# The last stage's product as three fp32r products, its operand split and stored as two halves

## The chip, the cores and the metric

One core of one Trainium2 chip runs the whole kernel in one launch. The metric is the time of one execution on the device in microseconds (us). Five engines work side by side, each through its own list of instructions in order, and wait for each other on semaphores: TensorE (PE in the profile, with PEld its weight loads), VectorE (DVE), ScalarE (ACT), GpSimd (POOL) and SyncE (SP), which here only starts transfers.

## The reference

All activations are float32, [2, 1024, 512]. Four blocks are added to `x` in turn:

```
x = x + attention_a(layernorm(x))     # 16 heads, filtered along time
x = x + ffn(layernorm(x))             # 8 experts of width 16, the best 2 of a softmax gate
x = x + attn_b(layernorm(x))
x = x + ffn(layernorm(x))             # the same weights again

def attn_b(X):
    h = layernorm(X) * ln_w + ln_b
    Q, K, V = split(h @ W_in + b_in)              # 512 each
    Q, K = rope(Q), rope(K)
    A = sum over time of (K / |K|) * V            # one row of 512 for each batch
    Y = A[:, None, :] * Q
    return Y @ W_out + b_out + X
```

The product of this document is `Y @ W_out`. Since `Y = A * Q`, the kernel forms `Q @ (diag(A) W_out)`: the 512x512 matrix `diag(A) W_out` is made once for each batch, when the sum over time is known.

## The kernel before

Three stages follow each other: `normalise`, `attention` and `tail`. Only `tail` is changed. The 2 x 1024 rows are cut into NT = 16 tiles of 128 rows (TB = 8 to a batch, KC = 4 blocks of 128 columns in 512).

`tail` is one software pipeline of 34 rounds, `for s in range(2 * NT + 2)`, written out for each engine in the order in which that engine runs it. In rounds 0 to 15 tile `t = s` of attention_a's output is multiplied with its weight and enters the first ffn; one to four rounds later the same tile passes through the ffn and attn_b's projections. In rounds 16 to 31 tile `s - 16` is multiplied with `diag(A) W_out` (`last_product`) and passes the second ffn. Rounds 16 to 19 hold both kinds of work, rounds 20 on only the second.

What one round does, with the lines of the profile:

- TensorE: transpose of the second norm of tile `s-3` (L1667); the product of tile `s` (L1594 through `product` for the first 16 tiles, L1650 for the last 16); transpose of the first norm (L1439) and of the gated hidden row (L1456); the experts down (L1448) and up (L1460); projections k and v (L1594); transpose of the rotated q of tile `s-4` into the PSUM bank `tq` (L1722); projection q (L1594). The transpose L1439 stands between the third and the fourth column block of `last_product`.
- VectorE: bias added to q (L1820); the low half of the second norm's transpose (`hTl`, L1826); the low half of the next input tile (`aTl`, L1745, up to round 14); `x`, the sum of the product and the residual (L1804), its statistics (L1353 to L1359); the first norm `n1` (L1374), which needs GpSimd's reciprocal root (L1363); the expert sum (L1411), its statistics; bias added to k (L1864); the gate (L1391 to L1403); the second norm `h2` (L1759); k times v (L1876); bias added to v (L1884). In rounds 13 and 21 the copy of A's columns (L1763) and four products `wout * acol` into `wab` (L1768) stand at the end (`columns`).
- GpSimd: rotation of q of tile `s-4` (L1998, L2000, L2001); the residual's bias (L2013) and its transfer to DRAM (L2015); the root for the first norm (L1363), and for the second (L2023); the root for |k| and the rotation of k; the sum over time (`summed`, L2038, or a copy L2035 at the first tile of a batch). In rounds 18 on it starts the output transfers (L2043).
- ScalarE: copies and casts out of PSUM (L1940, L1417, L1432, and the high half `aTh` L1929), the exponentials of the gate, the square of k (L1962), the residual for the last stage (L1972), the copy of `tq` into `qT` (L1981) and its transfer to DRAM (`qt_scratch`, L1983).
- SyncE: `load_tile`. For a tile of the last stage it loads the 256 KB of `qt_scratch` (L1548) and 256 KB of residual (L1550).

Up to round 19 a tile is loaded into one of two slots, from round 20 (`DEEP_AT`) into one of four, the other two of which are the buffers of q and k.

A projection is made of fp32r products: with operands x = xh + xl and w = wh + wl, `product` adds xh·wh, xl·wh and xh·wl (three matmuls for each of the four column blocks). `last_product` uses plain float32 operands, one matmul for each block, which shows in the trace as two instructions.

Of the kernel before, what the change touches and what calls it, by code (L numbers as in the profile page):

```python
# [237 lines left out]
def build(nc, a, out):  # L238
# [5 lines left out]
    qt_scr = nc.dram_tensor("qt_scratch", (NT, P, KC, P), F32, kind="Internal").ap()  # L244
    res_scr = nc.dram_tensor("res_scratch", (NT, P, E), F32, kind="Internal").ap()
    with ExitStack() as outer:
# [14 lines left out]
        with ExitStack() as ctx:  # L261
            def sb(name, shape, dt=F32):
# [4 lines left out]
                wab=place[:, 0:B * KC * E].rearrange("p (b c e) -> p b c e", b=B, c=KC),  # L267
# [1051 lines left out]
R = 4  # L1319
# [144 lines left out]
def tail(nc, a, x_tiles, out_tiles, att_scr, qt_scr, res_scr, w, late):  # L1464
    with ExitStack() as ctx:
# [8 lines left out]
        ident, wab, bout = w["ident"], w["wab"], w["bout"]  # L1474
# [6 lines left out]
        winh, winl = sb("winh", [P, KC, 3 * E], F32R), sb("winl", [P, KC, 3 * E], F32R)  # L1481
        aT = sb("aT", [P, 2, KC, P])
# [29 lines left out]
        s_res, s_fold2, s_col, s_acol, s_wab = (sem(n) for n in ("res", "fold2", "col", "acol", "wab"))  # L1512
# [4 lines left out]
        COLS_AT = (TB + 5, NT + 5)  # L1517
        DEEP_AT = NT + 4

        aTs = [aT[:, 0], aT[:, 1]] + [q[:, i].rearrange("p (c t) -> p c t", c=KC) for i in range(2)]  # L1520
# [5 lines left out]
        def loaded(t):  # L1526
            i = slot(t)
            uses = t // 2 if t < DEEP_AT else (DEEP_AT // 2 if i < 2 else 0) + (t - DEEP_AT) // R
            return s_in[i], 32 * uses + 32
# [6 lines left out]
        def _(sp):  # L1536
            def load_tile(t):
                if t >= DEEP_AT + R:
                    sp.wait_ge(ex.s_x, t - R + 1)
                elif t >= DEEP_AT + 2:  # L1540
                    sp.wait_ge(s_tq, NT)
                    sp.wait_ge(s_kv, NT)
                elif t >= 2:
                    sp.wait_ge(ex.s_x, t - 1)
                if t >= NT:
                    u = t - NT
                    sp.wait_ge(s_qTd[u % 2], u // 2 * 16 + 16)
                    sp.dma_start(aTs[slot(t)], qt_scr[u]).then_inc(s_in[slot(t)], 16)  # L1548
# [39 lines left out]
        def _(pe):  # L1588
# [53 lines left out]
            def last_product(s, rows):  # L1642
                if rows.start == 0:
                    pe.wait_ge(*loaded(s))
                    pe.wait_ge(s_wab, KC * ((s - NT) // TB + 1))
                    if s == DEEP_AT + 1:
                        pe.wait_ge(s_qb, NT)
                    pe.wait_ge(ex.s_x, s if wide(s) is wide(s - 1) else s - 1)
                for c in rows:
                    mm = mmul(wide(s)[:], aTs[slot(s)][:, c], wab[:, (s - NT) // TB, c], start=(c == 0), stop=(c == KC - 1))  # L1650
# [5 lines left out]
            for s in range(2 * NT + 2):  # L1656
# [12 lines left out]
                if NT <= s < 2 * NT:  # L1669
                    last_product(s, range(KC - 1))  # L1670
                if 0 <= s - 1 < 2 * NT:
                    ex.pe_turn(pe, s - 1, t0)
                if NT <= s < 2 * NT:
# [10 lines left out]
                elif s < NT:  # L1684
                    if s == WHOLE:
# [4 lines left out]
                            aTl[:, s % 2].rearrange("p c t -> p (c t)"), woh, wol, 0).then_inc(s_w, 1)  # L1690
                if s == 1:
# [25 lines left out]
                if 0 <= t < NT:  # L1717
                    pe.wait_ge(s_rq, 3 * t + 3)
                    if t >= 1:
                        pe.wait_ge(s_qT, t)  # L1720
                    for c in range(KC):
# [10 lines left out]
        def _(dve):  # L1732
# [28 lines left out]
            def columns(b):  # L1761
                dve.wait_ge(s_col, b + 1)
                vec.tensor_copy(acol[:, b], t1[:, 0:KC]).then_inc(s_acol, 1)  # L1763
                dve.wait_ge(s_acol, b + 1)
                if b == 0:
                    dve.wait_ge(s_wout, 16)
                for c in range(KC):
                    vec.tensor_scalar(wab[:, b, c], wout[:, c], acol[:, b, c:c + 1], None, ALU.mult).then_inc(s_wab, 1)  # L1768
# [45 lines left out]
            for s in range(2 * NT + 2):  # L1814
                t = s - 4
# [52 lines left out]
                if 0 <= t < NT:  # L1868
                    second_norm(t)
                t = s - 4  # L1870
# [26 lines left out]
        def _(act):  # L1897
# [32 lines left out]

            for c in range(2):
                high_weight(c)

            for s in range(2 * NT + 2):
# [18 lines left out]
                if s + 1 == WHOLE:  # L1953
                    round_a(WHOLE)
                if s == ROOT_AT:
# [19 lines left out]
                if 0 <= t < NT:  # L1975
# [3 lines left out]
                    if t >= 2:  # L1979
                        act.wait_ge(s_qTd[t % 2], t // 2 * 16)  # L1980
                    nc.scalar.copy(qT[:, t % 2].rearrange("p c t -> p (c t)"), tq[:]).then_inc(s_qT, 1)  # L1981
                    act.wait_ge(s_qT, t + 1)
                    act.dma_start(qt_scr[t], qT[:, t % 2]).then_inc(s_qTd[t % 2], 16)  # L1983
            for i in range(2):
                act.wait_ge(s_qTd[i], 16 * (NT // 2))
# [94 lines left out]
```

## Time and profile before

| | us |
|---|---|
| median of 3 runs | 1275.09 (1273.79 to 1275.57) |
| the profiled execution | 1279.85 |
| its span, first to last instruction | 1278.0 |
| round 3 to the end of round 19, about | 938 to 1188 |
| rounds 20 to 33, about | 1188 to 1278 |

The page of the profile shows shares over the whole span; the change touches only what runs after 900 us. The views used below are the busy time by window, the chain of work that ended last, the waits, and the timeline of single engines. In a timeline row the number in brackets is the time in which the engine sat idle before the instruction, with the engine and line that ended it.

### The profile page before, as it was taken

To read this page: it belongs to the slowest core of one execution; us is meant where nothing else is said; L and a number is where in the kernel's file an instruction comes from. 1 tells how busy PE (TensorE), PEld (TensorE's weight loads), DVE (VectorE), ACT (ScalarE), POOL (GpSimd) and SP (SyncE) were. 2 spreads that over 40 slices of the span, in tenths; PEclk is the share of its full clock that TensorE was granted. 3 is DMA by queue.
4 is the path that set the end of the run, shared out by engine and by line. 5 is a ranking of instruction groups with operands and counts; after the bars stand their busy time and mean duration, and the time that the engine had idled before them with its cause. 6 is when DMAs were issued, how large, how long until landed. Compare 5 with 4: busy or idle time off the path is not lost. (4 is left out here: it accounts for less than half of the span.)

```text
span 1278.0 us, 20694 instructions
## 1 busy us (share of the span) xinstructions
PE 1143.4 (89%) x7552; PEld 627.5 (49%) x7552; DVE 821.7 (64%) x1423; ACT 613.1 (48%) x1000; POOL 799.3 (63%) x586
## 2 busy tenths in 40 slices
PE   6999967999689899898898898898899999999995
PEld 5888622343233343243343333332467777777552
DVE  6886275667366557647646655650497788876885
ACT  4444225656556666566576565566442222222221
POOL 2012159579979879779698797776126666666211
PEclk9999969999899999999999998998999999999997
DMA  8333340120230220221212022004422312222431
GB/s 271 97 121 107 102 101 26 51 67 26 68 90 26 67 67 31 61 67 59 69 56 67 18 62 80 1 1 149 150 84 74 122 68 66 67 75 75 165 108 42
DMA packets 69956, 99.16 MB, mean 78 GB/s; under 512 B 12384, under 2 KB 35808, under 8 KB 69856
## 3 DMA queue, kind: packets, MB, share of 16 engines
q1 hardware_dynamic: 61024, 74.77, 20.2%
q0 software_dynamic: 4224, 14.68, 3.0%
q10 hardware_dynamic: 4608, 8.39, 1.8%
q8 instruction: 61, 1.00, 0.3%
q14 instruction: 39, 0.32, 0.1%
HBM read 64.25 MB, written 33.55 MB: 77 GB/s over the span
## 5 line engine op out<-in xcount | busy, mean ns | idle before, releaser
L1090 DVE TENSOR_REDUCE nm<-score 128x1 f32<-128x640 f32 (+6 forms) x352 | 349.5, 1026 | 272.8 <-PE score L981 222.4
L1257 POOL TENSOR_TENSOR base<-base,plain 128x2048 f32<-128x2048 f32 (+2 forms) x78 | 301.0, 3860 | 16.1 <-ACT plain L1206 6.2
L1206 ACT ACTIVATE plain<-score 128x1024 f32<-128x1024 f32 (+3 forms) x288 | 207.2, 734 | 108.2 <-PE score L997 61.2
L992 PE MATMUL score<-q,k 98*128 98x512 bf16 (+7 forms) x768 | 195.0, 340 | 51.0 <-ACT plain L1206 20.4
L1206 ACT ACTIVATE base<-score 128x1024 f32<-128x1024 f32 x96 | 97.5, 1023 | 72.8 <-PE score L997 51.4
L992 PEld LDWEIGHTS score<-q,k 98*128 98x128 bf16 (+1 forms) x768 | 54.8, 99 | 154.6 <-DVE nm L1090 57.7
L1010 PE MATMUL acc<-plain,vg 128*32 128x512 f32 (+3 forms) x1152 | 114.7, 471 | 0.0
L976 PE MATMUL score<-k,q 48*128 48x512 bf16 (+3 forms) x512 | 70.3, 354 | 17.7 <-DVE nm L1090 17.5
L1594 PE MATMUL m_b<-m_winh,m_hTh 128*128 128x512 f32 x192 | 83.7, 436 | 1.4 <-DVE m_k L1864 1.4
L1594 PE MATMUL m_b<-m_winh,m_hTl 128*128 128x512 f32 x192 | 75.9, 395 | 0.0
L1594 PE MATMUL m_b<-m_winl,m_hTh 128*128 128x512 f32 x192 | 75.7, 394 | 0.0
L997 PE MATMUL score<-mask_t,identb 128*128 128x128 bf16 x512 | 72.6, 224 | 0.0
L1283 POOL TENSOR_TENSOR num<-num,rden 128x512 f32<-128x512 f32 x16 | 20.3, 1268 | 76.6 <-ACT rden L1180 75.3
L1363 POOL TENSOR_TENSOR m_rstd<-m_rstd,m_half 128x1 f32<-128x1 f32 x32 | 18.0, 562 | 74.5 <-DVE m_rstd L1359 74.2
L997 PEld LDWEIGHTS score<-mask_t,identb 128*128 128x128 bf16 x512 | 49.3, 101 | 29.3 <-issue 6.1
L464 POOL TENSOR_SCALAR n_rstd<-n_mv 128x1 f32<-128x1 f32 x16 | 6.5, 406 | 83.5 <-DVE n_mv L426 83.5
L915 PE MATMUL misc<-base,ones 128*32 128x512 f32 x384 | 50.7, 632 | 8.0 <-POOL base L1257 7.5
L1010 PE MATMUL acc<-base,vg 128*32 128x512 f32 x384 | 53.7, 632 | 3.8 <-ACT num L1171 2.0
L1050 DVE TENSOR_TENSOR base<-base,plain 128x1536 f32<-128x1536 f32 (+1 forms) x30 | 49.9, 1662 | 0.1
L1178 ACT ACTIVATE rden<-misc 128x512 f32<-128x512 f32 x32 | 19.2, 599 | 59.0 <-PE misc L915 59.0
L962 PE MATMUL score<-k,q 48*128 48x128 bf16 (+3 forms) x256 | 36.0, 321 | 11.0 <-ACT plain L1206 3.7
L1424 ACT ACTIVATE m_e<-m_hl 128x128 f32<-128x128 f32 x32 | 8.9, 277 | 75.1 <-DVE m_top L1381 75.1
(253 smaller groups left out, 2491.6 us busy)
## 6 DMA issues: line engine op xcount, KB each, us to landing
q<-piece_scratch SPq DMA_DIRECT2D x192, 64.0 KB, 2.7
k<-piece_scratch SPq DMA_DIRECT2D x192, 64.0 KB, 2.2
piece_scratch<-n_pieces SPq DMA_DIRECT2D x16, 384.0 KB, 3.0
piece_scratch<-pieces POOLq DMA_DIRECT2D x8, 768.0 KB, 4.0
n_x1in<-in_query SPq DMA_DIRECT2D x16, 256.0 KB, 3.7
v_scratch<-n_v ACTq DMA_DIRECT2D x16, 256.0 KB, 2.1
vg<-v_scratch SPq DMA_DIRECT2D x8, 512.0 KB, 4.7
att_scratch<-m_qT SPq DMA_DIRECT2D x8, 512.0 KB, 3.0
```

Of the source, the lines that this page charges most:

```text
L915: mm = nc.tensor.matmul(misc[head * 2 * D:(head + 1) * 2 * D, t0:HALF], ones[:], tile_of(n, v)[:, head, t0:HALF], start=first, stop=last, ...
L962: nc.tensor.matmul(banks[odd][:, x], qst[n % SLOTS][c, head, i * P:width], kst[n % SLOTS][c, head, 0:width], start=(x == 0), stop=False, s ...
L976: nc.tensor.matmul(score[(k + odd) % RING][:, c0 // HALF, 0:c1 - c0], qst[n % SLOTS][c, heads[odd], i * P:width], kst[n % SLOTS][c, heads[ ...
L992: mm = nc.tensor.matmul(score[k % RING][:, x, t0:HALF], kst[n % SLOTS][c, first + x, j * P:(j + 1) * P], qst[n % SLOTS][c, first + x, h * ...
L997: mm = nc.tensor.matmul(score[k % RING][:, x, t0:t0 + P], identb[:], mask_t[:], start=False, stop=True, skip_group_check=True)
L1010: mm = nc.tensor.matmul(acc[x, t0:HALF], vg[:, n // 2 % 2, j, x], tile_of(n, v)[:, head, t0:HALF], start=(j == 0), stop=(j == (h + 1) * TB ...
L1050: nc.vector.tensor_tensor(total, total, tile_of(n, v)[:, :, t0:HALF], ALU.add).then_inc(s_add["dve"], 1)
L1090: nc.vector.tensor_reduce(out, src, AX.X, ALU.max, negate=True).then_inc(s_max, 1)
L1206: nc.scalar.activation(tile_of(n, v)[:, first:first + 2, t0:HALF], score[k % RING][:, :, t0:HALF], ACT.Exp)\
L1257: nc.gpsimd.tensor_tensor(total, total, tile_of(n, v)[:, :, t0:HALF], ALU.add)\
L1283: nc.gpsimd.tensor_tensor(num[:, h], num[:, h], rden[:, h], ALU.mult).then_inc(s_mul, 1)
L1594: mm = mmul(b[:], x[:, c * P:(c + 1) * P], y[:, c, col:col + E], start=(c == 0 and n == 0), stop=(c == KC - 1 and n == 2))
```

## The change

The 16 products of rounds 16 to 31 become fp32r products of three matmuls for each column block. For this both operands are split.

- The rows: ScalarE's copy of `tq` into `qT` rounds to fp32r (the high half). One round later VectorE forms `rest = tq - qT` (a new instruction at the start of rounds 5 to 20, ahead of L1820), and ScalarE starts a second transfer for it. `qt_scratch` holds two halves, and `load_tile` loads both, into `aTh`/`aTl` and `hTh`/`hTl` in place of `aT` and q.
- The weight: `columns` on VectorE keeps only the small copy. ScalarE makes the high halves (`high_columns`, four activations, in rounds 15 and 21), VectorE the low halves (`low_columns`, four scalar_tensor_tensor: all four in round 15 right after L1759, and two each at the end of rounds 21 and 22). The eight L1768 instructions are gone. The second set of columns is summed in round 20 instead of 21.
- The order: in round 16 `last_product` stands after the transposes in one piece; later rounds keep the split order.

```
@@ -241,7 +241,7 @@
...
     att_scr = nc.dram_tensor("att_scratch", (B * G, P, T), F32, kind="Internal").ap()
-    qt_scr = nc.dram_tensor("qt_scratch", (NT, P, KC, P), F32, kind="Internal").ap()
+    qt_scr = nc.dram_tensor("qt_scratch", (NT, 2, P, KC, P), F32, kind="Internal").ap()
     res_scr = nc.dram_tensor("res_scratch", (NT, P, E), F32, kind="Internal").ap()
@@ -264,7 +264,7 @@
...
                 down=sb("down", [P, KC, NX * IX + NX]), up=sb("up", [P, E]), bout=sb("bout", [P, E]),
-                wab=place[:, 0:B * KC * E].rearrange("p (b c e) -> p b c e", b=B, c=KC),
+                rest=place[:, 0:2 * E].rearrange("p (i e) -> p i e", i=2),
                 wout=place[:, B * KC * E:(B + 1) * KC * E].rearrange("p (c e) -> p c e", c=KC),
@@ -1471,7 +1471,7 @@
...
             return ctx.enter_context(nc.psum_tensor("m_" + name, [P, E], F32))
-        ident, wab, bout = w["ident"], w["wab"], w["bout"]
+        ident, bout, rest = w["ident"], w["bout"], w["rest"]
         ex = Experts(nc, ctx, "m_", w)
@@ -1479,6 +1479,7 @@
...
         winh, winl = sb("winh", [P, KC, 3 * E], F32R), sb("winl", [P, KC, 3 * E], F32R)
+        wabh, wabl = [woh, winh[:, :, 0:E]], [wol, winl[:, :, 0:E]]
         aT = sb("aT", [P, 2, KC, P])
@@ -1509,24 +1510,25 @@
...
         s_rk, s_rq, s_grown = sem("rk"), sem("rq"), sem("grown")
-        s_res, s_fold2, s_col, s_acol, s_wab = (sem(n) for n in ("res", "fold2", "col", "acol", "wab"))
+        s_res, s_fold2, s_col, s_acol, s_wabh, s_wabl = (sem(n) for n in ("res", "fold2", "col", "acol", "wabh", "wabl"))
+        s_rest = sem("rest")
         s_resd = [sem(f"resd{i}") for i in range(R)]
...
         NCONST, NCONSTB, NROPED = 4, 2, 4
-        COLS_AT = (TB + 5, NT + 5)
+        COLS_AT = (TB + 5, NT + 4)
         DEEP_AT = NT + 4
-
-        aTs = [aT[:, 0], aT[:, 1]] + [q[:, i].rearrange("p (c t) -> p c t", c=KC) for i in range(2)]
+        LOW_COLS_AT = {COLS_AT[1] + 1: (0, 1), COLS_AT[1] + 2: (2, 3)}
+
+        qts = [[pair[:, i].rearrange("p (c t) -> p c t", c=KC) if pair in (hTh, hTl) else pair[:, i] for pair in pairs
+                for i in range(2)] for pairs in ((aTh, hTh), (aTl, hTl))]
         xins = [xin[:, 0], xin[:, 1], k[:, 0], k[:, 1]]
...
         def loaded(t):
-            i = slot(t)
-            uses = t // 2 if t < DEEP_AT else (DEEP_AT // 2 if i < 2 else 0) + (t - DEEP_AT) // R
-            return s_in[i], 32 * uses + 32
+            return s_in[slot(t)], sum(32 if u < NT else 48 for u in range(t + 1) if slot(u) == slot(t))
 
@@ -1538,14 +1540,15 @@
...
                 elif t >= DEEP_AT + 2:
-                    sp.wait_ge(s_tq, NT)
+                    sp.wait_ge(s_q, NT)
                     sp.wait_ge(s_kv, NT)
...
                     u = t - NT
-                    sp.wait_ge(s_qTd[u % 2], u // 2 * 16 + 16)
-                    sp.dma_start(aTs[slot(t)], qt_scr[u]).then_inc(s_in[slot(t)], 16)
+                    sp.wait_ge(s_qTd[u % 2], u // 2 * 32 + 32)
+                    for n in range(2):
+                        sp.dma_start(qts[n][slot(t)].bitcast(F32), qt_scr[u, n]).then_inc(s_in[slot(t)], 16)
                     sp.wait_ge(s_resd[u % R], u // R * 16 + 16)
@@ -1640,14 +1643,17 @@
...
             def last_product(s, rows):
+                b = (s - NT) // TB
                 if rows.start == 0:
                     pe.wait_ge(*loaded(s))
-                    pe.wait_ge(s_wab, KC * ((s - NT) // TB + 1))
+                    pe.wait_ge(s_wabl, KC * (b + 1))
                     if s == DEEP_AT + 1:
...
                     pe.wait_ge(ex.s_x, s if wide(s) is wide(s - 1) else s - 1)
+                (xh, xl), wh, wl = (half[slot(s)] for half in qts), wabh[b], wabl[b]
                 for c in rows:
-                    mm = mmul(wide(s)[:], aTs[slot(s)][:, c], wab[:, (s - NT) // TB, c], start=(c == 0), stop=(c == KC - 1))
+                    for n, (x, y) in enumerate(((xh, wh), (xl, wh), (xh, wl))):
+                        mm = mmul(wide(s)[:], x[:, c], y[:, c], start=(c == 0 and n == 0), stop=(c == KC - 1 and n == 2))
                 return mm
@@ -1666,11 +1672,11 @@
...
                     mm.then_inc(s_t2, 1)
-                if NT <= s < 2 * NT:
+                if NT < s < 2 * NT:
                     last_product(s, range(KC - 1))
...
                     ex.pe_turn(pe, s - 1, t0)
-                if NT <= s < 2 * NT:
+                if NT < s < 2 * NT:
                     last_product(s, range(KC - 1, KC)).then_inc(s_w, 1)
@@ -1688,6 +1694,8 @@
...
                             aTl[:, s % 2].rearrange("p c t -> p (c t)"), woh, wol, 0).then_inc(s_w, 1)
+                if s == NT:
+                    last_product(s, range(KC)).then_inc(s_w, 1)
                 if s == 1:
@@ -1718,6 +1726,7 @@
...
                         pe.wait_ge(s_qT, t)
+                        pe.wait_ge(s_rest, t)
                     for c in range(KC):
@@ -1761,11 +1770,12 @@
...
                 vec.tensor_copy(acol[:, b], t1[:, 0:KC]).then_inc(s_acol, 1)
-                dve.wait_ge(s_acol, b + 1)
-                if b == 0:
-                    dve.wait_ge(s_wout, 16)
-                for c in range(KC):
-                    vec.tensor_scalar(wab[:, b, c], wout[:, c], acol[:, b, c:c + 1], None, ALU.mult).then_inc(s_wab, 1)
+
+            def low_columns(b, part):
+                for c in part:
+                    dve.wait_ge(s_wabh, b * KC + c + 1)
+                    vec.scalar_tensor_tensor(wabl[b][:, c], wout[:, c], acol[:, b, c:c + 1], wabh[b][:, c].bitcast(F32),
+                                             ALU.mult, ALU.subtract).then_inc(s_wabl, 1)
 
@@ -1812,6 +1822,13 @@
...
             for s in range(2 * NT + 2):
+                t = s - 5
+                if 0 <= t < NT:
+                    dve.wait_ge(s_qT, t + 1)
+                    if t >= 2:
+                        dve.wait_ge(s_qTd[t % 2], t // 2 * 32)
+                    vec.tensor_tensor(rest[:, t % 2].bitcast(F32R), tq[:], qT[:, t % 2].rearrange("p c t -> p (c t)"),
+                                      ALU.subtract).then_inc(s_rest, 1)
                 t = s - 4
@@ -1867,6 +1884,10 @@
...
                     second_norm(t)
+                if s == NT - 1:
+                    low_columns(0, range(KC))
+                elif s in LOW_COLS_AT:
+                    low_columns(1, LOW_COLS_AT[s])
                 t = s - 4
@@ -1927,6 +1948,17 @@
...
                 nc.scalar.copy(aTh[:, t % 2], aT[:, t % 2]).then_inc(s_aTh, 1)
+
+            def high_columns(b):
+                act.wait_ge(s_acol, b + 1)
+                if b == 0:
+                    act.wait_ge(s_wout, 16)
+                    act.wait_ge(s_w, NT)
+                else:
+                    act.wait_ge(s_q, NT)
+                for c in range(KC):
+                    nc.scalar.activation(wabh[b][:, c], wout[:, c], ACT.Copy, scale=acol[:, b, c:c + 1])\
+                        .then_inc(s_wabh, 1)
 
@@ -1952,6 +1984,8 @@
...
                     round_a(WHOLE)
+                if s in (NT - 1, COLS_AT[1] + 1):
+                    high_columns(int(s > NT))
                 if s == ROOT_AT:
@@ -1977,12 +2011,17 @@
...
                     if t >= 2:
-                        act.wait_ge(s_qTd[t % 2], t // 2 * 16)
-                    nc.scalar.copy(qT[:, t % 2].rearrange("p c t -> p (c t)"), tq[:]).then_inc(s_qT, 1)
+                        act.wait_ge(s_qTd[t % 2], t // 2 * 32)
+                    nc.scalar.copy(qT[:, t % 2].rearrange("p c t -> p (c t)").bitcast(F32R), tq[:]).then_inc(s_qT, 1)
                     act.wait_ge(s_qT, t + 1)
-                    act.dma_start(qt_scr[t], qT[:, t % 2]).then_inc(s_qTd[t % 2], 16)
+                    act.dma_start(qt_scr[t, 0], qT[:, t % 2]).then_inc(s_qTd[t % 2], 16)
+                t = s - 5
+                if 0 <= t < NT:
+                    act.wait_ge(s_rest, t + 1)
+                    act.dma_start(qt_scr[t, 1], rest[:, t % 2].rearrange("p (c t) -> p c t", c=KC))\
+                        .then_inc(s_qTd[t % 2], 16)
             for i in range(2):
-                act.wait_ge(s_qTd[i], 16 * (NT // 2))
+                act.wait_ge(s_qTd[i], 32 * (NT // 2))
 
...
         def _(pool):

```

## Rows read from the trace of the kernel before

**Rows 1.** Busy time by window: from:to, length, PE PEld DVE ACT POOL busy, clock, DMA share, GB/s.

```profile
1051.17:1065.80 14.63, 14.60 (x73) 11.58 (x72) 11.64 (x31) 4.29 (x11) 10.13 (x12) 1.00 0.21 73
1095.04:1111.82 16.78, 15.65 (x82) 12.87 (x81) 13.89 (x36) 4.29 (x11) 10.13 (x12) 1.00 0.19 63
...
1126.11:1140.35 14.24, 14.24 (x65) 10.18 (x64) 10.95 (x29) 3.98 (x10) 9.74 (x12) 1.00 0.18 60
1140.35:1154.87 14.52, 14.52 (x66) 10.40 (x66) 10.95 (x30) 3.98 (x10) 9.74 (x12) 1.00 0.19 57
1154.87:1169.92 15.05, 15.05 (x69) 10.83 (x68) 11.07 (x30) 3.97 (x10) 9.74 (x12) 1.00 0.25 69
...
1213.90:1225.82 11.92, 11.79 (x48) 6.41 (x47) 9.73 (x34) 2.75 (x10) 2.29 (x4) 1.00 0.38 132
```

**Rows 2.** The chain that ended last, in round 10: start us, us, engine, tile, line.

```profile
1057.70 0.60 DVE m_v L1876
...
1058.97 1.29 POOL m_summed L2038
...
1065.80 0.55 DVE m_n L1374
...
1072.33 0.59 DVE m_v L1876
```

**Rows 3.** Waits between 950 and 1130 us: who for whom, us in total, times, longest.

```profile
PEld m_t L1667 <- DVE m_h L1759: 6.1, 11, 1.0
```

**Rows 4.** Timeline of VectorE (DVE), rounds 10, 13, 14 and 15: start us, us, instruction.

```profile
1059.37 0.67 DVE L1820 TENSOR_TENSOR m_q<-m_b,m_bin 128x512 f32<-128x512 f32 x1
1059.96 0.67 DVE L1826 TENSOR_TENSOR m_hTl<-m_t,m_hTh 128x512 fp32r<-128x512 f32 x1
...
1103.40 2.17 DVE L1768 TENSOR_SCALAR raws<-raws,m_acol 128x512 f32<-128x512 f32 x4
1105.49 0.68 DVE L1820 TENSOR_TENSOR m_q<-m_b,m_bin 128x512 f32<-128x512 f32 x1
...
1132.56 1.23 DVE L1876 SCALAR_TENSOR_TENSOR m_v<-m_k,m_rinv,m_v 128x512 f32<-128x512 f32 x1
```

**Rows 5.** Timeline of GpSimd (POOL), rounds 10 and 14.

```profile
1060.22 0.74 POOL L1998 TENSOR_TENSOR m_sw<-m_q,m_rope 128x256 f32<-128x256 f32 x1
...
1106.25 0.74 POOL L1998 TENSOR_TENSOR m_sw<-m_q,m_rope 128x256 f32<-128x256 f32 x1 [2.15 <-DVE m_q L1820]
```

**Rows 6.** Line L2000 on GpSimd: ns min/median/max, first and last start.

```profile
L2000 POOL TENSOR_TENSOR m_q<-m_q,m_rope x16: 724/1058/1155, 958.6 to 1179.8; 128x256 f32<-128x256 f32 x16
```

**Rows 7.** The chain on TensorE: an fp32r projection, and six float32 instructions of a product.

```profile
1130.18 2.79 PE m_b L1594 x12
...
1148.44 2.58 PE m_bw L1650 x6
```

**Rows 8.** Timelines of VectorE and TensorE at the start of round 18.

```profile
1160.86 0.54 DVE L1759 TENSOR_SCALAR m_h<-m_x,m_mv,m_rr 128x512 f32<-128x512 f32 x1
...
1162.89 0.60 PE L1667 MATMUL m_t<-ident,m_h 128*128 128x128 f32 x4
```

**Rows 9.** Timeline of VectorE in rounds 19 to 23.

```profile
1187.85 0.75 DVE L1876 SCALAR_TENSOR_TENSOR m_v<-m_k,m_rinv,m_v 128x512 f32<-128x512 f32 x1
1188.51 0.68 DVE L1804 TENSOR_TENSOR m_x<-m_bw,m_xin 128x512 f32<-128x512 f32 x1
...
1200.21 0.16 DVE L1763 COPY m_acol<-m_t 128x4 f32<-128x4 f32 x1
...
1202.00 0.68 DVE L1804 TENSOR_TENSOR m_x<-m_bw,m_k 128x512 f32<-128x512 f32 x1
...
1207.79 0.69 DVE L1804 TENSOR_TENSOR m_x<-m_b,m_k 128x512 f32<-128x512 f32 x1
```

**Rows 10.** Two lines of ScalarE (ACT): ns min/median/max, first and last start.

```profile
L1983 ACTq DMA_DIRECT2D qt_scratch<-m_qT x16: 326/326/327, 970.8 to 1185.0; - x16
...
L1972 ACT ACTIVATE raws<-m_x,m_shift,m_grow x16: 815/817/819, 938.5 to 1161.0; 128x512 f32<-128x512 f32 x16
```


## The prediction

> **What bounds the kernel now.** I read the busy time by window first, because the change touches only the tail. In rounds 5 to 15 one round takes 14.63 us, in rounds 20 on two take 11.92 [rows 1]. TensorE is busy nearly throughout in both, but its matmuls are pipelined, so I asked the chain and the waits who really sets the pace.
>
> In the middle rounds the chain does not pass through TensorE. It goes from k times v on VectorE (1057.70) to the sum over time on GpSimd (1058.97), on through the rotation of q, the residual's bias and transfer and the root, back to VectorE's first norm (1065.80) and down VectorE's list to the next k times v (1072.33): 14.63 us later, exactly a round [rows 2]. TensorE waits in each of these rounds for the second norm, 6.1 us in 11 waits [rows 3]. So in rounds 5 to 15 a loop over VectorE and GpSimd is the bound. Without the `aTl` subtraction that loop takes 14.24 us (round 15 to 16). Rounds 16 to 17 take 14.52 and 17 to 18 take 15.05, for here TensorE carries the float32 product beside the projections [rows 1]. The second norm is over at 1161.40 and TensorE begins round 18 only at 1162.89 [rows 8]: it has the lead there, by 1.49 us.
>
> In rounds 20 on two bounds lie close together. VectorE alone, with the next `x` right at the end of its list, takes 5.79 us (1202.00 to 1207.79) [rows 9]; two rounds take 11.92, thus 5.96 each [rows 1].
>
> **The products.** Six float32 instructions take 2.58 us, so the eight of a tile take 3.44; the twelve fp32r matmuls of a projection, of the same shapes as the new product, take 2.79 [rows 7]. I take 0.65 us off each tile. The Trainium skill, FP8 and Floating Point Precision, "TensorE Precision Notes", says that true float32 makes four passes through the array; three for four would be 2.58 us instead of 3.44, 0.86 off instead of 0.65. The measured fp32r product decides here.
>
> Rounds 16 and 17: bound by VectorE and GpSimd after the change (below), so nothing is gained. Rounds 18 and 19: 2 x 0.65 = 1.30 off.
>
> **The subtraction `rest`, rounds 5 to 20.** It reads one operand in PSUM and one in SBUF, as L1826 does, whose neighbour starts 0.59 before it [rows 4]: 0.60 us each. It stands ahead of q's bias, and GpSimd's rotation of q waits for that. In round 10 q's bias is over at 1060.04 and the rotation starts at 1060.22; in round 14, where it hangs on q's bias alone, it starts 0.08 after it (1105.49 + 0.68 to 1106.25) [rows 4, 5]. The slack is therefore 0.10, and 0.50 of the 0.60 goes into the loop. What could give the 0.10 back is L2000, which runs 1.06 us mostly and up to 1.15 [rows 6]. I take 0.55 for each of rounds 5 to 13: nine times, +4.95. The idle 2 us in which VectorE waits for the root are no cover, since the root comes later by the same amount.
>
> ScalarE's second transfer costs it 0.33 us of issue [rows 10] in a round where it is busy 4.29 of 14.63 [rows 1]; I put it at nothing. If this cover were gone, `hTh` and `aTh` would come later and with them `hTl`, 0.3 us a round.
>
> **Columns of the first batch.** Four L1768 took 2.09 us (1103.40 to 1105.49) just ahead of q's bias in round 14 [rows 4]. They go: -2.09 + 0.60 = -1.49. Round 15: +0.50; round 16: +0.53 by the same count.
>
> The four `low_columns` of round 15 stand between the second norm and k times v, inside the loop. The trace has no such operation; the nearest is L1876, also a scalar_tensor_tensor of 128x512 from SBUF, 0.75 us long with the next instruction 0.66 after it [rows 9]. In the middle rounds it takes 1.23 [rows 4]. That forced wait now falls on the first of the four and leaves k times v. So 4 x 0.66 = +2.64. Bounds: 2.15 if nobody waits any more, 4.6 if all four take the long form. ScalarE's four high halves, at most 0.82 each [rows 10], follow its exponentials and have VectorE's work from the first norm to the second, some 6 us, to end in; ScalarE is busy 3.98 of 14.24 [rows 1]: at nothing. Without that cover up to 3.3 us would be added once. TensorE waits for them in round 16, which is no loss, for the loop is later still.
>
> The Trainium skill, SBUF — State Buffer, "Who interferes with whom", says that a VectorE instruction with two SBUF inputs contends with a GpSimd instruction that reads SBUF, and one with a single SBUF input does not. By that `rest` is never held up and the low halves may be; the 1.23 beside 0.75 agrees [rows 4, 9].
>
> **Rounds 17 to 19.** The loop takes 14.24 + 0.53 = 14.77 where 14.52 stood: +0.25. Sum until the second norm of round 17: 4.95 - 1.49 + 0.50 + 0.53 + 2.64 + 0.25 = +7.38. TensorE had 1.49 us in hand [rows 8]: +5.89 at its start of round 18. The two shorter products take off 1.30: +4.59 at `x` of round 19.
>
> **Columns of the second batch.** From `acol` to the next `x` it was 1.79 us (1200.21 to 1202.00), with VectorE working without a pause [rows 9]. Now: `acol` 0.18, `rest` 0.60, four low halves 2.64: 3.42, so +1.63. Bounds 1.4 to 2.1. Sum +6.22.
>
> **Rounds 23 to 31.** TensorE's part shrinks by 0.65 in a cycle of two rounds, 11.92 - 0.65 = 11.27, but VectorE's list allows no less than 2 x 5.79 = 11.58 [rows 1, 9]. I take 5.80 for 5.96 in eight rounds: -1.26. Bounds 0 and -2.6 (eight times 0.325). The loads grow from 512 to 768 KB a round, where the DMA engines are busy 0.38 of the time [rows 1]; tiles are fetched four rounds ahead, so nothing. The granted clock is 1.00 here; TensorE would idle some 0.4 us a round, and it kept 1.00 through round 13, where it is busy 15.65 of 16.78 [rows 1].
>
> **The sum.** 6.22 - 1.26 = +4.96 us on the profiled execution's 1279.85, with the same difference on the median of 1275.09: 1280.05 us, 0.39% slower. With all low bounds (0.50 a round, low halves 2.15, 1.4, -2.6) it is +2.4; with all high ones (0.68 a round, 4.6, 2.1, 0) +10.4: 1277.5 to 1285.4.
>
> **The rivals.**
>
> *The subtraction is hidden.* `rest` falls into a time in which GpSimd isn't ready for q anyway. Then only round 14's -2.09 counts in the middle rounds, TensorE keeps the lead from 16 on: it waits some 2.0 us for the low halves of round 15 and gains 4 x 0.65, then +1.03 for the second columns and -1.26: -2.9, or 1272.2 us. It decides if the sum over time ends 0.60 us or more after q's bias is over. Against it: that distance is 0.10 [rows 4, 5]. For it: only that the chain is inferred. Chance 0.11.
>
> *TensorE is the bound.* Busy 14.60 of 14.63 [rows 1], each of 16 tiles gives back 0.65: -10.4, 1264.7 us. Against it: the wait for the second norm in each round [rows 3]. By the skill's passes (FP8 and Floating Point Precision, "TensorE Precision Notes") it would be 16 x 0.86, 1261.3 us. Chance 0.06.
>
> *VectorE waits for GpSimd at the new instructions.* If `rest` takes what L1876 takes beside a GpSimd instruction, 0.48 more (1.23 for 0.75) [rows 4, 9], eleven rounds give +5.3, and low halves at 4.6 another 1.96: +12.2, up to 1287.3 us; half of it 1283.7. Against it: q's bias, likewise with one PSUM operand, takes 0.67 while GpSimd sums [rows 2, 4]. Chance 0.10.
>
> *The forecast*: 0.73.
>
> **How the numbers follow.** The predicted time is the forecast's, 1280.05. A change under 0.2% (2.55 us) can hardly be told from none here. The forecast's own range is 1277.5 to 1285.4, with some 0.06 of its 0.73 below +2.55. For 8 in 10 I take 1276.5 to 1286.5: this leaves out the hidden subtraction (0.11), TensorE as the bound (0.06) and about 0.03 of the rest. Slower: 0.67 + 0.10 = 0.77. Within 0.2%: 0.06 and half of the hidden case, 0.12. Faster: 0.06 and the other half, 0.11.
>
> **What would show it.** In the changed kernel's profile: rounds 6 to 12 take 15.1 to 15.2 us instead of 14.63, with L1998 released by q's bias in all of them and TensorE's waits for the second norm near 1 us; round 13 to 14 takes near 15.3 instead of 16.78; the low halves of round 15 take near 2.7 us on VectorE, and TensorE waits for them in round 16; two rounds after 24 take 11.6 with VectorE without a pause. The prediction is wrong if rounds 6 to 12 stay at 14.63, or if VectorE still idles ahead of L1804 in the last rounds.

## The result, and the profile after

| | before | after |
|---|---|---|
| median | 1275.45 us (1273.79 to 1277.65, 7 runs) | 1281.67 us (1279.31 to 1285.21, 7 runs) |
| ratio, 95% interval | | 1.0047 (1.0032 to 1.0063) |
| profiled execution / its span | 1279.85 / 1278.0 | 1280.19 / 1278.4 |

The change costs 6.0 us (4.1 to 8.0). The two profiled executions hardly differ (0.4 us in their spans), because the one of before spent 3.58 us more ahead of the changed stage: the first L1374 starts at 914.11 there and at 910.53 after. So all shifts below are counted from that instruction: time of an event minus time of the first L1374, after minus before. "Round 10" is the time from the first norm of round 10 to that of round 11, and so on.

In the changed kernel these lines have new numbers: rotation of q L2037, L2039, L2040 (was L1998 to L2001), q's bias L1837 (L1820), k times v L1897 (L1876), sum over time L2077 (L2038), `x` L1814 (L1804), transpose of the second norm L1673 (L1667), last product L1656 (L1650). L1830 is `rest`, L1777 `low_columns`, L1960 `high_columns`.

Busy time by window in the profile after, from one first norm to the next (columns as in [rows 1]): round 10; rounds 13, 14, 15 and 16; two rounds from the `x` of round 24.

```profile
1050.50:1065.61 15.11, 14.58 (x73) 11.57 (x72) 12.14 (x32) 4.29 (x11) 10.18 (x12) 1.00 0.25 88
1096.10:1111.30 15.20, 13.57 (x74) 11.18 (x73) 12.47 (x33) 4.30 (x11) 10.16 (x12) 1.00 0.19 68
1111.30:1126.08 14.78, 14.78 (x74) 12.01 (x73) 11.53 (x30) 4.51 (x12) 9.82 (x12) 1.00 0.34 120
1126.08:1143.55 17.47, 16.05 (x79) 12.82 (x78) 14.20 (x34) 5.50 (x13) 9.87 (x12) 1.00 0.33 112
1143.55:1158.33 14.78, 14.25 (x70) 11.04 (x69) 11.52 (x31) 3.98 (x10) 9.83 (x12) 1.00 0.30 105
...
1216.24:1227.83 11.59, 10.69 (x54) 7.89 (x54) 9.71 (x34) 2.75 (x10) 2.29 (x4) 1.00 0.54 182
```

Read the first number behind each window against [rows 1]: 15.11 for 14.63 in the middle rounds, 15.20 for 16.78 where the old column products went, 17.47 for 14.24 where the low halves are, 14.78 for 14.52 in the next, and 11.59 for 11.92 at the end. TensorE's busy time in round 10 did not move (14.58 for 14.60), although the round is 0.48 longer.

The chain that ended last, in the same part of round 10 as [rows 2]:

```profile
1057.02 0.93 DVE m_v L1897
...
1058.08 0.68 DVE m_v L1905
1058.76 0.60 DVE raws L1830
1059.36 0.61 DVE m_q L1837
...
1060.03 0.75 POOL m_sw L2037
...
1065.61 0.55 DVE m_n L1374
```

Before, the chain left VectorE with k times v and went on through the sum over time on GpSimd. Now it stays on VectorE through v's bias, `rest` and q's bias, and only then goes to GpSimd. The sum over time has dropped out of the chain. In the timelines of the same stretch, VectorE first and then GpSimd:

```profile
1058.68 0.68 DVE L1830 TENSOR_TENSOR raws<-m_tq,m_qT 128x512 fp32r<-128x512 f32 x1
1059.28 0.67 DVE L1837 TENSOR_TENSOR m_q<-m_b,m_bin 128x512 f32<-128x512 f32 x1
...
1065.61 0.55 DVE L1374 TENSOR_SCALAR m_n<-m_x,m_mv,m_rstd 128x512 f32<-128x512 f32 x1 [2.46 <-POOL m_rstd L1363]
```

```profile
1058.29 1.30 POOL L2077 TENSOR_TENSOR m_summed<-m_summed,m_v 128x512 f32<-128x512 f32 x1 [0.68 <-POOL m_k L2040]
1060.03 0.74 POOL L2037 TENSOR_TENSOR m_sw<-m_q,m_rope 128x256 f32<-128x256 f32 x1 [0.44 <-DVE m_q L1837]
```

`rest` puts 0.60 us between v's bias and q's bias. GpSimd is through with the sum at 1059.59 and stands idle 0.44 us until q's bias is over. That idle time is nearly all of the round's loss, 0.48; VectorE itself idles 2.46 us ahead of the norm and gains nothing from it. The waits from 950 to 1130 us say it for all rounds (columns as in [rows 3]). First the line of before: GpSimd waited for q's bias in 4 places there, in 12 now.

```profile
POOL m_sw L1998 <- DVE m_q L1820: 6.1, 4, 2.9
...
POOL m_sw L2037 <- DVE m_q L1837: 9.2, 12, 2.9
PEld m_t L1673 <- DVE m_h L1768: 8.6, 9, 1.0
```

The low halves, on VectorE in round 15:

```profile
1132.53 3.22 DVE L1777 SCALAR_TENSOR_TENSOR m_wol<-raws,m_acol,m_woh 128x512 fp32r<-128x512 f32 x4
1135.68 0.74 DVE L1897 SCALAR_TENSOR_TENSOR m_v<-m_k,m_rinv,m_v 128x512 f32<-128x512 f32 x1
```

The four occupy VectorE for 3.15 us up to k times v; k times v itself takes 0.74 there where it took 1.23 [rows 4]. So they cost about 2.66. The product that waits for them, on TensorE:

```profile
1135.85 0.47 PE L1656 MATMUL m_bw<-m_woh,m_aTh 128*128 128x512 f32 x1 [1.42 <-issue]
1136.16 0.40 PE L1656 MATMUL m_bw<-m_woh,m_aTl 128*128 128x512 f32 x1
...
1138.47 0.40 PE L1656 MATMUL m_bw<-m_wol,m_aTh 128*128 128x512 f32 x1
```

The trace names no releaser (`<-issue`), but the wait ends 0.10 us after the last low half (1132.53 + 3.22 = 1135.75). The twelve matmuls start 0.23 to 0.24 apart, but for the first.

### The profile page after: what moved, and what is told of

It reads as the page before. It is cut to its first block and busy times, and to the rows that moved or that the text cites. A ratio compares the mean times of both kernels' runs of the same rounds, so it can differ in the third digit from the quotient of the medians.

```text
span 1278.4 us, 20880 instructions
## 1 busy us (share of the span) xinstructions
PE 1131.9 (89%) x7601; PEld 637.8 (50%) x7616; DVE 832.5 (65%) x1439; ACT 617.5 (48%) x1008; POOL 799.9 (63%) x586
## 3 DMA queue, kind: packets, MB, share of 16 engines
q10 hardware_dynamic: 6912, 12.59, 2.6%
## 5 line engine op out<-in xcount | busy, mean ns | idle before, releaser
L1374 DVE TENSOR_SCALAR m_n<-m_x,m_mv,m_rstd 128x512 f32<-128x512 f32 x32 | 17.5, 546 | 44.6 <-POOL m_rstd L1363 44.6
```

The lines of the kernel that those rows point to most:

```text
L1374: self.nc.vector.tensor_scalar(self.n1[:, t % 2], self.x[:, t % R], self.mv[:, t % R, 0:1], self.rstd[:, t % R], ALU.subtract, ALU.mult).t ...
```

## The experiments

Medians and ratios below are against runs of the kernel before on the same chip. Shifts and lengths of rounds are each from one profiled execution, and shifts are against the profile before, counted from the first L1374.

**The subtraction elsewhere on VectorE (rest_gap).** The block with `rest` goes from the start of the round to between the row maximum (L1381) and the first norm, where VectorE waits for the root anyway.

```
+                t = s - 5
+                if 0 <= t < NT:
...
+                    vec.tensor_tensor(rest[:, t % 2].bitcast(F32R), tq[:], ...)
                 if s < 2 * NT:
                     ex.dve_norm(dve, s)
```

> The changed kernel with one edit: the subtraction stands between the gate's maximum and the first norm, where VectorE idles 2.5 us for GpSimd's root, instead of ahead of q's bias. Loop theory (the subtraction costs because GpSimd's rotation of q waits behind it): rounds 6 to 12 back to 14.63 us, round 13 to 14 near 14.7, TensorE has the lead again in rounds 17 to 19; 2.4 us under the kernel before, about 1272.5 us, some 7 us under the changed one. Rival (VectorE's total work sets the round): nothing changes, rounds 15.1 us, about 1281 us. Rival (TensorE sets the round): nothing changes either.

Measured: 1274.86 us (1272.08 to 1276.76, 12 runs), ratio 0.9971 (0.9955 to 0.9987): faster than before by 3.7 us. The changed kernel was not run beside it; by the two ratios rest_gap is some 10 us faster. The changed stage itself shows less: its last `x` comes 1.49 us ahead of before, 6.4 ahead of the changed kernel (1.49 + 4.94), where 2.4 and some 7 were expected. Where the runs gain the rest is not shown. Rounds 5 to 10 take 14.63 or 14.64 each, round 11 takes 14.86, and round 13 takes 14.99 where 14.7 was expected. Round 10 by window:

```profile
1048.92:1063.55 14.63, 14.59 (x73) 11.55 (x72) 12.59 (x31) 4.30 (x11) 10.13 (x12) 1.00 0.26 93
```

VectorE is busy even longer than in the changed kernel (12.59 for 12.14), TensorE and GpSimd the same, and the round is back at its old length. What the subtraction costs is its place. A second set of runs (rest_gap_again, with split_low below) gave 1274.51, ratio 0.9970 (0.9957 to 0.9983).

> The kernel with the subtraction alone moved, once more, on the same chip as the one that also splits the low halves: 0.2 to 0.3% below before, rounds 6 to 11 at 14.63 us.

**The subtraction alone (before_rest).** The kernel before plus the one new instruction in its place at the start of the round. Its result is used by nothing; only TensorE and ScalarE wait for it before they write over what it reads. Products, columns and transfers stay as before.

```
+                    vec.tensor_tensor(rest, tq[:], qT[:, t % 2].rearrange("p c t -> p (c t)"),
+                                      ALU.subtract).then_inc(s_rest, 1)
```

> The kernel before with one part of the change alone: the subtraction (its result unused) ahead of q's bias in rounds 5 to 20; products, transfers and columns as before. Loop theory: +0.5 us in each of rounds 5 to 17, TensorE's lead of 1.49 us in round 18 taken off, +0.6 in round 20: about +5.5 us, 0.43% slower than before, rounds 6 to 12 at 15.1 us. Rival (TensorE sets the round, the subtraction is hidden): within 0.2% of before.

Measured: 1284.04 us (1280.28 to 1287.6, 12 runs), ratio 1.0042 (1.0024 to 1.006), thus +5.4.

```profile
1049.42:1064.53 15.11, 14.58 (x73) 11.56 (x72) 12.20 (x31) 4.30 (x11) 10.17 (x12) 1.00 0.20 70
```

The same 15.11 as in the changed kernel. At the first norm of round 13 it is 4.74 us behind (the changed kernel 4.64), at the second norm of round 17 6.6 and at the last `x` 6.2. One instruction of 0.6 us makes up the middle rounds' whole loss.

**The subtraction behind q's bias (rest_after_q).** Two lines moved past each other: L1837 first, then `rest`.

> The subtraction stands right behind the bias added to q instead of right ahead of it; nothing else differs from the changed kernel. Loop theory (what counts is only that GpSimd's rotation of q starts later): the rotation starts as early as before, so rounds 6 to 12 go back to near 14.63 us (at most 14.8, if the later hTl, x and first norm matter), and the whole is some 4.5 us shorter than the changed kernel, near the kernel before or a little below. Rival, VectorE's total work is the bound: rounds 6 to 12 stay at 15.1 us and the time stays 6 us above before.

Measured: 1277.37 us (1273.68 to 1282.03, 10 runs), ratio 0.9997 (0.9978 to 1.0016). Rounds 5 to 10 take 14.64, but for round 8 with 15.75:

```profile
1023.91:1039.66 15.75, 15.40 (x75) 11.93 (x74) 13.36 (x31) 4.29 (x11) 9.80 (x12) 1.00 0.22 77
1054.30:1068.94 14.64, 14.57 (x73) 11.55 (x72) 12.49 (x31) 4.30 (x11) 10.14 (x12) 1.00 0.26 92
```

The last `x` comes 0.11 us behind before and 4.83 ahead of the changed kernel, for the 4.5 that were expected. The rival, VectorE's total work, is out: its list has the same instructions, and a round takes 0.47 us less. The odd round is told under the hardware, below.

**Without the second transfer (one_transfer).** Second store and second load are left out, with the waits for them, so that the low half that the product reads is not q's.

```
-                    for n in range(2):
-                        sp.dma_start(qts[n][slot(t)].bitcast(F32), qt_scr[u, n])...
+                    sp.dma_start(qts[0][slot(t)].bitcast(F32), qt_scr[u, 0])...
...
-                    act.dma_start(qt_scr[t, 1], rest[:, t % 2]...)
```

> Leaves out the second store of each middle round and the second load of each tile of the last stage, so the low half of q is not the one the product needs; the arithmetic instructions are all there. Theory (the transfers are hidden): no difference from the changed kernel beyond 0.5 us: rounds 6 to 12 at 15.1, rounds from 24 on at 5.8, 0.4 to 0.5% above before. Rival, the doubled traffic or the second issue on ScalarE costs time: rounds 6 to 12 or the rounds from 24 on become shorter by 0.1 us or more each, together 1.5 us or more.

Measured: 1282.68 us (1279.57 to 1287.24, 10 runs), ratio 1.0039 (1.0021 to 1.0057).

```profile
1057.18:1072.30 15.12, 14.59 (x73) 11.57 (x72) 12.21 (x32) 4.29 (x11) 10.16 (x12) 1.00 0.20 71
```

Round 10 takes 15.12, and the last `x` is 5.15 us behind instead of 4.94. The doubled traffic and the second issue cost nothing that shows.

**Without the low halves of round 15 (no_low0).** The four instructions are left out, and TensorE waits for the high halves instead, so the first batch is multiplied with a wrong low half.

```
-                if s == NT - 1:
-                    low_columns(0, range(KC))
-                elif s in LOW_COLS_AT:
+                if s in LOW_COLS_AT:
```

> The changed kernel without the four low halves of round 15; the first batch's products use stale low weights. Loop theory: the first norm of round 16 comes 2.7 us earlier against that of round 15, and all of it stays until round 31, since GpSimd and VectorE keep the lead: span of the tail 2.7 us shorter, TensorE's 1.6 us wait in round 16 gone. Rival (the low halves only fill time in which something else is waited for): under 1 us.

Measured (a single execution, 1283.88 us; its changed stage starts 4.2 us later than in the profile after, so only lengths are read):

```profile
1131.54:1146.31 14.77, 14.77 (x74) 12.01 (x73) 11.53 (x31) 5.74 (x14) 9.81 (x12) 1.00 0.35 120
```

14.77 for 17.47: the four cost 2.70 us in the loop. It all stays to the end, as expected: this kernel was 1.24 us behind the changed one at the norm of round 14, mostly by the clock (below), and is 1.43 ahead of it at the last `x`, 2.67 gained.

**Two matmuls for three (two_products).** `last_product` leaves out the product with the weight's low half.

```
-                    for n, (x, y) in enumerate(((xh, wh), (xl, wh), (xh, wl))):
+                    for n, (x, y) in enumerate(((xh, wh), (xl, wh))):
```

> The changed kernel with two matmuls for three in each column block of the last product (high rows times low weight left out), 0.93 us less TensorE work a tile. Loop theory: only rounds 18 and 19 and at most a trifle in 17 are bound by TensorE, so 0.9 to 1.9 us in all; rounds 24 to 31 stay at 5.80 us. Rival (TensorE sets the pace of the last stage): 16 x 0.93 = 15 us, or some 11 us for the twelve rounds from 20 on.

Measured (a single execution, 1284.33 us, changed stage 5.3 us late): the norm of round 18 to that of round 19 takes 10.98 for 12.32 us, 1.34 less. The two rounds ahead of that keep their 14.77 or 14.78, and in rounds 24 to 31 nothing moves (5.80 each). A product shorter by 0.9 us is worth something only between these two norms; in the other rounds of the last stage TensorE is not what the round waits for.

**The low halves spread (spread).** On top of rest_gap: low halves in the gap ahead of the first norm, two in round 15 and one each in rounds 21, 22 and 23; the high halves of blocks 0 and 1 ahead of the exponentials instead of behind them.

```
+        LOW_GAP = {NT - 1: (0, (0, 1)), COLS_AT[1] + 1: (1, (0,)), COLS_AT[1] + 2: (1, (1,)),
+                   COLS_AT[1] + 3: (1, (3,))}
...
+                if s in LOW_GAP:
+                    low_columns(*LOW_GAP[s])
                 if s < 2 * NT:
                     ex.dve_norm(dve, s)
```

> The subtraction stands in VectorE's idle time ahead of the first norm, and of the eight low halves five stand there too: two of the first batch in round 15 (the other two stay behind the second norm), and one each of the second batch in rounds 21, 22 and 23 (the remaining one at the end of round 22). Theory: against the kernel with the subtraction alone moved, round 15 to 16 is 1.3 us shorter, since only two low halves stand in the loop, and the second columns cost some 0.8 us instead of 2.7, because in rounds 20 on VectorE idles 0.6 us ahead of each first norm; together 3 us less: 0.45% below before. If the idle time is no cover (the low halves are held up by GpSimd, or the first norm comes later by their length), it stays at 0.2 to 0.3% below.

Measured: 1276.48 us (1272.23 to 1278.96, 12 runs), ratio 0.9985 (0.9968 to 1.0002). This expectation fell: it is no better than rest_gap. In round 15 there was no gap to fill, since `x` comes late there and the root is ready when `rest` is over: 1.3 us less in one round came back as 1.3 more in the other. In rounds 21 to 23 there was a gap, and it helped by 0.4 us from the `x` of round 20 to that of round 24, not by the 1.9 expected. VectorE, and GpSimd's root beside it:

```profile
1202.08 0.74 DVE L1778 SCALAR_TENSOR_TENSOR m_winl<-raws,m_acol,m_winh 128x512 fp32r<-128x512 f32 x1
1203.29 0.55 DVE L1374 TENSOR_SCALAR m_n<-m_x,m_mv,m_rstd 128x512 f32<-128x512 f32 x1 [0.46 <-POOL m_rstd L1363]
```

```profile
1202.16 1.08 POOL L1363 TENSOR_TENSOR m_rstd<-m_rstd,m_half 128x1 f32<-128x1 f32 x1 [3.18 <-DVE m_rstd L1359]
...
1215.46 0.56 POOL L1363 TENSOR_TENSOR m_rstd<-m_rstd,m_half 128x1 f32<-128x1 f32 x1 [3.17 <-DVE m_rstd L1359]
```

The root takes 1.08 us beside a low half and 0.56 without. The gap is the root's time, and the work put into it holds up the root. The next run asks whether any work does this or only work of this kind.

**The same with one operand in PSUM (spread_psum).** For the second batch the low halves subtract what is in the bank `tq`, so the last eight tiles are multiplied with other numbers.

```
-    ... acol[:, b, c:c + 1], wabh[b][:, c].bitcast(F32), ...
+    ... acol[:, b, c:c + 1], tq[:] if b else wabh[b][:, c].bitcast(F32), ...
```

> As the kernel with the low halves spread, but the four low halves of the second batch subtract what lies in the PSUM bank tq instead of the high half in SBUF: they have one operand in SBUF, not two, and the last eight tiles' values are not the reference's. Theory (VectorE's instruction with two SBUF operands held up GpSimd's root, 1.08 us instead of 0.56 in rounds 21 to 23): the root takes 0.56 us again in those rounds, the first norm starts 2.50 us after x instead of 3.03, and from the x of round 20 to that of round 24 it is 1.5 us shorter. Rival, any work of VectorE placed there delays the norm: root and norm stay as they were.

Measured (a single execution), VectorE and GpSimd:

```profile
1197.85 0.74 DVE L1778 SCALAR_TENSOR_TENSOR m_winl<-raws,m_acol,m_tq 128x512 fp32r<-128x512 f32 x1
1198.53 0.55 DVE L1374 TENSOR_SCALAR m_n<-m_x,m_mv,m_rstd 128x512 f32<-128x512 f32 x1
```

```profile
1197.93 0.56 POOL L1363 TENSOR_TENSOR m_rstd<-m_rstd,m_half 128x1 f32<-128x1 f32 x1 [3.17 <-DVE m_rstd L1359]
```

An instruction of the same length at the same place, and the root takes 0.56 and the norm follows at once. From `x` to the norm it is 2.51 or 2.52 us in rounds 21 to 23, for 3.02 to 3.04 in spread. From the `x` of round 20 to that of round 24 it is 1.15 us less than in spread, not 1.5: TensorE makes `x` of round 24 wait 0.46.

**The low halves split (split_low).** On top of rest_gap: two low halves stay behind the second norm of round 15, two go behind q's bias in round 16.

```
+                    if s == NT:
+                        low_columns(0, (2, 3))
...
-                    low_columns(0, range(KC))
+                    low_columns(0, (0, 1))
```

> As the kernel with the subtraction moved ahead of the first norm, but only two of the first batch's low halves stand behind the second norm in round 15; the other two follow q's bias in round 16, behind which GpSimd's rotation of q starts, and the product of round 16 waits for each block by itself. Theory (the loop over GpSimd counts only what stands ahead of q's bias): the round from first norm 15 to 16 falls from 16.95 to some 15.6 us, x of round 16 comes no later by more than 0.3, and the whole is 1.3 us shorter: 0.3 to 0.4% below before. Rival, the low halves cost 0.66 us each wherever they stand, since hTl and x come later: 16.95 stays.

Measured: 1275.68 us (1271.88 to 1279.99, 12 runs), ratio 0.9982 (0.9968 to 0.9997); rest_gap beside it 1274.51. This expectation fell too: the round from norm 15 to 16 takes 16.39 for 16.95, not 15.6. GpSimd's rotation of q in that round:

```profile
1131.31 1.18 POOL L2041 TENSOR_TENSOR m_sw<-m_q,m_rope 128x256 f32<-128x256 f32 x1
1132.56 1.06 POOL L2043 TENSOR_TENSOR m_q<-m_q,m_rope 128x256 f32<-128x256 f32 x1
```

In rest_gap these take 0.74 and 0.73. They are 0.77 us longer, and of the 1.35 that was expected 0.79 is missing: the two low halves, with both operands in SBUF, ran beside the rotation (1131.04 to 1133.03). Of the 0.56 that was left nothing arrived at the last `x`: split_low is 0.27 us ahead of rest_gap_again there (1.66 and 1.39 ahead of before), and it was so already at the norm of round 15 (1.77 and 1.50). Round 18 takes 13.57 for 13.03, for from there on TensorE has the lead. So rest_gap stays the best version.

## Why the prediction was right

Time and range held: 1280.05 forecast, 1281.67 measured, and slower. Its steps, from the profile pair:

| by | forecast | measured |
|---|---|---|
| first norm of round 13 (nine times 0.55) | +4.95 | +4.64 |
| first norm of round 14 | +3.46 | +3.06 |
| first norm of round 16 | +7.13 | +6.78 |
| first norm of round 17 | +7.38 | +7.04 |
| TensorE's start of round 18 (transpose of the second norm) | +5.89 | +5.60 |
| `x` of round 19 | +4.59 | +4.45 |
| `x` of round 23 | +6.22 | +6.24 |
| `x` of round 31 | +4.96 | +4.94 |
| end | +4.96 | +3.98 |

The mechanism held at each step. That the last `x` came within 0.02 of the forecast is in part luck: the rounds up to the norm of round 14 cost 0.40 less than forecast, while rounds 18 and 19 gave back 0.20 less and the second columns cost 0.16 more.

- *The loop.* Right, and shown twice: by before_rest, where the instruction alone makes 15.11 of 14.63, and by rest_gap and rest_after_q, where it costs nothing. Its size was 0.48 to 0.51 in eight of the nine rounds, for 0.55: the lower bound, the 0.60 less a slack of 0.10, was nearly exact, and the 0.05 added for a possible lengthening of L2000 was not needed (its successor L2039 takes 1.06 as before). Round 11 alone lost 0.74. It is about 0.24 longer than its neighbours in every variant but one_transfer, before_rest too; why is not shown. The prediction's "rounds 5 to 15" at 14.63 us before is too wide: rounds 4 to 12 take it, and 13, 14 and 15 take 16.78, 14.29 and 14.24. Its sum treats these apart.
- *Low halves of round 15.* 2.64 forecast, 2.70 by no_low0. The long form left k times v (0.74) for the low halves: the four take 3.15 us to the next start, 0.51 above 4 x 0.66. In spread and split_low the first two behind the second norm take 1.88 and 1.89 us, two in the gap 1.41, so it fell on one of the first two. ScalarE's four high halves are over at 1127.80, the low halves start at 1132.53: at nothing was right.
- *The product.* From the first of the twelve matmuls to the start of the last it is 2.62 us, and with the last 2.85: nearer to the 2.79 read from the projection than to the 2.58 beside it.
- *Rounds 16 to 19.* The loop holds through 17, TensorE leads from 18 on; two_products shows the turn: nothing in rounds 16 and 17, and 1.34 us between the norms of rounds 18 and 19.
- *The last rounds.* 11.59 for two, as VectorE's list allows (11.58). That TensorE's relief goes beyond that is shown by two_products: shorter still, no change. The clock stayed at 1.00 there with TensorE busy 10.69 of 11.59 us, as forecast. But the other comfort, that it kept 1.00 through round 13, did not hold in every execution: see the clock, below.
- *Transfers at nothing.* one_transfer confirms it within what its runs can tell.
- *The rivals.* "The subtraction is hidden" fell with the 0.44 us that GpSimd idles each round. "TensorE is the bound" fell with round 10's TensorE time, which stayed at 14.58 while the round grew, and for the last stage with two_products; no run shortens TensorE's work in the middle rounds. "VectorE waits for GpSimd at the new instructions" fell for `rest`: it takes 0.60 to the next instruction beside the sum on GpSimd. The low halves cost 2.70, not that rival's 4.6.

What was not forecast is the last 1.0 us of the profile, between the last `x` and the end: 22.55 us before, 21.59 after. The record speaks against an effect of the change. before_rest, whose last rounds are those of the kernel before, takes 21.47 there, and the others lie between 20.55 and 22.52. So the pair's +4.94 at the last `x` is the better reading of the change, and the runs' +6.0 (4.1 to 8.0) agrees with it. The clock's fall and the long issue told below come in some executions and not in others and can add to such a difference; no run shows how often they come.

## What to carry to other kernels

Find the loop that sets the length of a round before pricing an edit: TensorE was busy 14.60 of 14.63 us in the middle rounds, yet 0.6 us more on VectorE lengthened each of them by 0.5; and in rounds 16 and 17, where it was busy throughout before, a product shorter by 0.9 us was worth nothing after the change. A new instruction costs by its place in its engine's order: behind the hand-over to the next engine of the loop it was free, ahead of it it cost nearly all its length in each round. And a gap on one engine may be another engine's working time: what is put into it must not hold that one up, so work with one operand in PSUM was the better filling here.

## What the hardware did that was not expected

**A VectorE instruction holds up a tiny one of GpSimd.** The root works on 128x1, yet took 1.08 us instead of 0.56 when a low half, with two SBUF operands, had started 0.08 us before it; it ended 0.42 us after the low half. With one operand in PSUM it took 0.56. The Trainium skill, SBUF — State Buffer, "Who interferes with whom", says that a VectorE instruction with two SBUF inputs contends with a GpSimd instruction that reads SBUF, and that the order of issue decides which of the two is held up. These rows agree: the low half started first and the root was held up. It ended 0.42 after the low half, less than its own 0.56, so not all of it came behind. The prediction had used the rule only for GpSimd holding up VectorE.

**The clock between the norms of rounds 13 and 14.** TensorE waits there for the copy of A's columns, 1.63 us (1.10 in spread). In three of the ten profiles of kernels in which ScalarE and VectorE make the columns' halves (two_products, no_low0, spread) its granted clock then fell to 0.50, the level of 1.2 GHz, for some 3 us. two_products by window; TensorE is busy 0.84 of 1.50 us before the fall and 0.53 in the window in which it comes:

```profile
1107.49:1108.99 1.50, 0.84 (x9) 0.75 (x7) 1.50 (x3) 1.28 (x2) 1.03 (x2) 1.00 0.00 0
1108.99:1110.49 1.50, 0.53 (x3) 0.56 (x4) 1.50 (x5) 0.00 (x0) 1.21 (x1) 0.66 0.51 188
1110.49:1111.99 1.50, 1.50 (x9) 1.50 (x8) 0.81 (x2) 0.63 (x2) 0.88 (x3) 0.50 0.48 172
1111.99:1113.49 1.50, 1.50 (x6) 1.22 (x6) 0.65 (x2) 1.22 (x3) 1.38 (x2) 0.70 0.00 0
```

The round then took 16.35 instead of 15.20 us (16.60 instead of 14.99 in spread). The profile after has the same wait of 1.63 us and the same busy times in the first two windows, 0.84 and 0.53, and its clock stays at 1.00. What decides it is not shown.

**The second issue behind the first.** ScalarE's first transfer of a round is issued in 0.33 us in every profile; the one right behind it takes 0.44 mostly, and up to 1.83. The line in rest_after_q (ns min/median/max):

```profile
L2021 ACTq DMA_DIRECT2D qt_scratch<-raws x16: 327/444/1832, 987.8 to 1192.8; - x16
```

The long one, between the norms of rounds 8 and 9, delayed `hTh` and `hTl`. `aTl`, a subtraction with two SBUF operands, then started beside GpSimd's bias of the residual and took 1.81 us for 1.04, `x` came late, and the round took the 15.75 above. rest_gap, spread and split_low have a long one of 1.44, 1.10 and 1.26 us, in round 19 and without a loss that shows, rest_after_q another of 1.40 in round 15; the changed kernel's profile has none. Why it comes is open.
